# Group 0's low-part subtraction moved from VectorE to GpSimd in three of four wide expert stages

## The reference

```python
def _L2_ffn_ref(x, router_w, w1, w2, w3):        # _L3_ffn_ref is the same
    ...
    topk_probs, topk_idx = jax.lax.top_k(probs, TOP_K)      # 2 of 8 experts
    ...
    h1 = jnp.einsum('nc,ehc->neh', flat, w1)     # 64 -> 682
    h3 = jnp.einsum('nc,ehc->neh', flat, w3)
    h = jax.nn.silu(h1) * h3
    y = jnp.einsum('neh,ech->nec', h, w2)        # 682 -> 64
    out = jnp.einsum('ne,nec->nc', gates, y)
```

## Time and profile before

| | |
|---|---|
| median of 3 runs | 2331.3 us (2331.04 to 2332.63) |
| the profiled execution, its own time | 2329.65 us |
| its span | 2327.8 us |
| mean granted TensorE clock | 0.812 of full speed |
| DVE / PE / ACT / POOL busy | 74% / 68% / 58% / 43% |
| `y_done` waits of POOL (L602) | 449.3 us in 136 waits |

### The profile page before, as it was taken

The page is one execution under the profiler, slowest core; times in us unless marked ns, Lnnn a source line. Parts: engine busy times, 40 slices in busy tenths (PEclk is TensorE's granted clock), DMA queues, the critical chain, the costliest instruction groups (busy, mean ns, idle before and its releaser), DMA issues.

```text
span 2327.8 us, 50752 instructions
## 1 busy us (share of the span) xinstructions
PE 1580.9 (68%) x16748; PEld 1179.4 (51%) x16749; DVE 1718.9 (74%) x2892; ACT 1354.8 (58%) x2460; POOL 1006.3 (43%) x955
## 2 busy tenths in 40 slices
PE   4367777778676767657777912699913099977995
PEld 3344444435343433336667811688802088866884
DVE  3567668776877587547778867788867588869886
ACT  0256655677778676765656711477701277766774
POOL 1023334432223122871223478144477577754443
PEclk8578767778898677997888955799955599989997
DMA  7000000000002000000000010010020211110012
GB/s 300 0 25 1 1 25 1 1 1 1 1 1 76 23 1 5 21 26 15 17 16 22 22 59 22 20 28 27 20 84 22 91 36 34 34 63 23 26 29 88
DMA packets 53028, 76.25 MB, mean 33 GB/s; under 512 B 14905, under 2 KB 37642, under 8 KB 50206
## 3 DMA queue, kind: packets, MB, share of 16 engines
q1 hardware_dynamic: 30658, 43.26, 6.1%
q0 software_dynamic: 22208, 30.81, 3.8%
HBM read 40.89 MB, written 35.19 MB: 33 GB/s over the span
## 4 chain that ended last, share of the span: by engine, by line
PE 32%; DVE 17%; issue 6%; POOL 5%; ACT 2%; DMA 2%; POOLq 0%; SPq 0%; ACTq 0%; DVEq 0%
PE bank L1607 12%; PE bank L1608 9%; PE bank L1621 5%; POOL rows L578 3%; DVE tmp L1067 2%; PE bank L1623 2%; PE bank L1593 1%; DVE act L1227 1%; DVE hl L1231 1%; PE bank L1372 1%; POOL x L616 1%; PE bank L1503 1%; ACT act L774 1%; DVE tmp L1045 1%; DVE st L892 1%
## 5 line engine op out<-in xcount | busy, mean ns | idle before, releaser
L602 POOL DMA_INDIRECT y<-ysb,ids x352 | 394.8, 1122 | 522.6 <-DVE ysb L1218 449.3
L616 POOL TENSOR_TENSOR x<-x,ysb 128x256 f32<-128x256 f32 x288 | 267.4, 928 | 665.6 <-DVE ysb L1305 657.3
L756 ACT ACTIVATE hb<-bank,bias_sb 128x512 f32<-128x512 f32 x432 | 298.6, 691 | 244.2 <-issue 141.6
L578 POOL DMA_INDIRECT rows<-rowsb,pos x288 | 333.1, 1156 | 103.6 <-issue 74.6
L1607 PE MATMUL bank<-xT,gA 128*114 128x256 f16 x1056 | 330.6, 313 | 59.8 <-DVE act L1227 28.5
L1227 DVE TENSOR_TENSOR act<-bank,act 114x512 f32<-114x512 f32 x352 | 241.5, 686 | 162.9 <-ACT act L774 162.2
L774 ACT ACTIVATE act<-bank 114x512 f32<-114x512 f32 x352 | 210.2, 597 | 235.1 <-PE bank L1608 232.1
L1608 PE MATMUL bank<-xT,gB 128*114 128x256 f16 x1056 | 298.7, 283 | 0.0
L1607 PE MATMUL bank<-xT,uA 128*114 128x256 f16 x1056 | 298.1, 282 | 0.0
L1608 PE MATMUL bank<-xT,uB 128*114 128x256 f16 x1056 | 298.1, 282 | 0.0
L1621 PE MATMUL bank<-dW,hl 114*128 x2112 | 259.8, 224 | 7.0 <-DVE hl L1231 6.1
(11 more groups left out here) (239 smaller groups left out, 3371.2 us busy)
## 6 DMA issues: line engine op xcount, KB each, us to landing
xs<-rows SPq DMA_DIRECT2D x176, 65.0 KB
stage<-up SPq DMA_DIRECT2D x8, 1368.0 KB, 6.8
rows<-land POOLq DMA_DIRECT2D x8, 1137.5 KB, 17.8
y<-ysb,ids POOLq DMA_INDIRECT x352, 2.2
rows<-rowsb,pos POOLq DMA_INDIRECT x288, 2.4
stage<-down SPq DMA_DIRECT2D x2, 1368.0 KB
rowsb<-y SPq DMA_DIRECT2D x4, 640.0 KB, 6.2
rows<-land POOLq DMA_DIRECT2D x4, 585.0 KB, 20.6
```

The lines of the kernel that those rows point to most:

```text
L578: pool.indirect_dma_start(rows_d[l - SPARSE][h], bass.IndirectOffsetOnAxis(pos[h][:, k, j:j + 1], 0), words(h)[:, j * RW // 2:(j + 1) * RW ...
L602: pool.indirect_dma_start(y_d[h], bass.IndirectOffsetOnAxis(ids[h][:, t * SUB + u:t * SUB + u + 1], 0), ysb[t % UNROLL][:, u * C:(u + 1) * ...
L616: pool.tensor_tensor(xv, xv, tg[u % 2], ALU.add).then_inc(s["added"], 1)
L756: ins = a.activation(dst[:, 0:SPAN * P], PB[w % 3][:, :], ACT.Gelu, scale=1.0 / WSCALE, bias=b1T[l][:, at:at + 1])
```

## The change

In the stages (2,0), (2,1) and (3,1), not in (3,0), `low` of group 0 is no longer on DVE. POOL does it, in `back`: tiles 0 and 1 ahead of everything, tile t + 2 behind the two transfers of tile t. A new semaphore `helped` counts these; `silu` and `down23` of group 0 wait on it, and the counts of `hp_ready` shrink accordingly.

```diff
+        HELPED = [(2, 0), (2, 1), (3, 1)]
+        def on_pool(l, h, g):
+            return g == 0 and (l, h) in HELPED
+        def low_ready(eng, l, h, i, k, g):
+            if on_pool(l, h, g):
+                wait_from(eng, s["helped"], i * UNROLL + (help_base(l, h) + k + 1))
+            else:
+                n = lows(l, h)
+                wait_from(eng, s["hp_ready"], i * (UNROLL * n) + (split_base(l, h) + k * n + g + 1 - (SPLIT - n)))
...
             def back(l, h, aside, early):
...
+                def low(t):
+                    if on_pool(l, h, 0) and t < TILES:
+                        pool.wait_ge(s["hi_ready"], (tile_base(l, h) + t) * SPLIT + 1)
+                        pool.tensor_tensor(hl[0][0:CH, 2 * ROWS:4 * ROWS], hold(0, 0)[0:CH, :], hl[0][0:CH, 0:2 * ROWS],
+                                           ALU.subtract).then_inc(s["helped"], 1)
+                low(0)
+                low(1)
                 for t in range(TILES):
...
                     pool.wait_ge(s["y_done"], tile_base(l, h) + t + 1)
                     for u in range(SUB):
                         pool.indirect_dma_start(y_d[h], bass.IndirectOffsetOnAxis(ids[h][:, t * SUB + u:t * SUB + u + 1], 0),
...
+                    low(t + 2)
...
                 def silu(i, k, g):
-                    wait_from(a, s["hp_ready"], i * (UNROLL * SPLIT) + (sb_ + (k - 1) * SPLIT + g + 1))
+                    if not (isinstance(i, int) and i == 0 and k == 0):
+                        low_ready(a, l, h, i, k - 1, g)
...
                 def low(i, k, g):
-                    v.wait_ge(s["hi_ready"], i * (UNROLL * SPLIT) + (sb_ + k * SPLIT + g + 1))
+                    if on_pool(l, h, g):
+                        return
+                    v.wait_ge(s["hi_ready"], i * (UNROLL * SPLIT) + (hb_ + k * SPLIT + g + 1))
...
                 def down23(i, k, g, e):
-                    pe.wait_ge(s["hp_ready"], i * (UNROLL * SPLIT) + (split_base(l, h) + k * SPLIT + g + 1))
+                    low_ready(pe, l, h, i, k, g)
```

More of the change, by code:

```diff
@@ L339, in program @@
                  "bias_ld b_done l1b_ps w01_done b2_ld b2_moved "
-                 "split_lo xt_ps xt_done cnt_ps cnt_read gain_read res_read up_ps gelu_done lo_ready down_ps gated added").split()
+                 "split_lo xt_ps xt_done cnt_ps cnt_read gain_read res_read up_ps gelu_done helped lo_ready down_ps gated added").split()
         s = {n: sem(n) for n in names}
@@ L419, in middle, with lows, help_base @@
                 body(i)
-        def split_base(l, h):
-            return m_of(l, h) * TILES * SPLIT
+        HELPED = [(2, 0), (2, 1), (3, 1)]
+        def on_pool(l, h, g):
+            return g == 0 and (l, h) in HELPED
+        def lows(l, h):
+            return sum(not on_pool(l, h, g) for g in range(SPLIT))
+        def split_base(l, h):
+            return sum(TILES * lows(*divmod(m + SPARSE * HALVES, HALVES)) for m in range(m_of(l, h)))
+        def help_base(l, h):
+            return sum(TILES * (SPLIT - lows(*divmod(m + SPARSE * HALVES, HALVES))) for m in range(m_of(l, h)))
+        def low_ready(eng, l, h, i, k, g):
[4 more added lines that the diff above has]
+                wait_from(eng, s["hp_ready"], i * (UNROLL * n) + (split_base(l, h) + k * n + g + 1 - (SPLIT - n)))
         def hold(k, g):
@@ L764, in moe @@
                 gb, tb = group_base(l, h), tile_base(l, h)
-                sb_ = split_base(l, h)
                 plan = inner(l, h)
@@ L1219, in evict @@
                     ins.then_inc(s["y_done"], 1)
-                sb_ = split_base(l, h)
+                hb_ = m_of(l, h) * TILES * SPLIT
                 def product(i, k, g):
```

## The result

| | before | after |
|---|---|---|
| median of 5 runs, taken beside each other | 2331.3 us (2330.26 to 2332.63) | 2546.63 us (2538.64 to 2549.79) |
| the profiled execution, its span | 2329.65, 2327.8 us | 2546.9, 2545.1 us |
| mean granted TensorE clock | 0.812 | 0.803 |

The changed kernel takes 1.0918 times as long (95% interval 1.0903 to 1.0934), 215 us more. 2553 was forecast.

What follows compares the result with a forecast made beforehand. TensorE was taken to set the pace in the three undisturbed stretches, 485.6 us for 101 tiles. A POOL loop of 7.0 us a tile makes 707, 221 more; 2331.3 + 221 gives 2553 us, range 2496 to 2645.

Steps and rivals of the forecast that it cites:

- The loop: Three wide stages: POOL's subtraction, silu, product, eviction and both transfers run once per tile, 7.0 us against 4.66 to 4.93.
- The estimate for the subtraction: POOL's subtraction of 114 x 512 elements, estimated at 1.3 us, with ends of 0.74 and 1.90.
- leaving the exclusion out of the sum: POOL's and DVE's subtractions excluding one another: 0.37 us a tile, 7.37 and 2590 us, not taken.
- an even distance: In (2,1) and (3,1), starts of the first transfers should stand 7.0 us apart, evenly.
- The longer fourth tile: Each fourth tile's pause of some 1.3 us should fall into time in which engines wait for POOL.
- The sum: Undisturbed stretches of three stages: 101 tiles x 7.0 = 707 us in place of 485.6, so 221 more.
- Two terms set at zero: First part of (2,0): 7.3 us lacking against at most 8 won, zero; stage (3,0): keeps its length.
- DVE's relief: First part of (2,0), where DVE can be late: 14 x 0.60 = 8 us at most.
- The dearer operation: Rival: POOL's subtraction costs 1.9 us or more, giving 2613, and 2664 at 2.4 us; chance 0.12.
- The clock: Rival: TensorE falls to 1.2 GHz, 8.8 us a tile; 2735 for all 101 tiles, 2644 for half; chance 0.09.
- The loop that doesn't close: Rival: POOL's 3.9 us a tile fit into 4.66 and are hidden; time stays at 2331; chance 0.04.
- The faster case: Rival: POOL's work hidden and DVE's relief counts in the first part of (2,0), 8 us, 2323; chance 0.03.

Runs made afterwards that it cites:

- e10_lean: Against e1_ahead: `helped` rises by 3 a tile and `hp_ready` by 2 for group 1, so wait values are those of the kernel before; 2338.05 us.
- e9_counts_only: Against the kernel before: only the change's semaphores and counts, DVE still does all subtractions in the old order; 2347.31 us.
- e1_ahead: Against the changed kernel: POOL's subtraction of tile t + 2 moved ahead of the wait for `y_done` of tile t, TensorE given its own wait; 2355.62 us.
- e3_twice: Against the changed kernel: POOL's subtraction behind the transfers done twice, first into a spare tile; 2680.74 us.
- e2_between: Against the changed kernel: POOL's subtraction of tile t + 2 placed between the two transfers of tile t; 2417.16 us.
- e6_idle_work: Against the kernel before: POOL also subtracts constants into a spare tile behind the transfers in the same three stages, nobody waiting for it; 2428.13 us.
- e6w_write_only: Against e6_idle_work: a memset of 114 x 1024 fp16, which reads nothing, in place of the useless subtraction; 2338.03 us.

## Why the prediction was right

**What bounds the kernel.** Right: TensorE sets the pace before. e10_lean shows it: DVE's busy time in (2,1) fell by 20.8 us, and the stretch didn't get shorter. What the prediction left out is that TensorE's pace has an issue part: nine register operations more a pass lengthen (3,0) by 6.1 us in after and by 7.5 in e9_counts_only.

**The loop.** Right, and shown from both sides: opened, the same work costs 26 us, and 6 with lean counts (e1_ahead, e10_lean); lengthened by 1.11 us it costs 134 us more (e3_twice); shortened by one transfer and a gap it gives tiles of 5.24 (e2_between). The rows of POOL, ScalarE, DVE and TensorE follow each other as the prediction walked through them.

**Its terms.** 7.0 was forecast, 6.53 is the clean turn:

| term | forecast | measured |
|---|---|---|
| silu to product | 0.63 | 0.62 |
| product to the eviction's end | 1.63 | 1.63 |
| eviction to transfer | 0.77 | 0.77 |
| two transfers | 2.56 | 2.28 |
| transfer to subtraction | 0.03 | 0.00 |
| subtraction | 1.3 | 1.19 |
| handing on to silu | 0.10 | 0.04 |

The largest miss is in the transfers: the first one, 1.28 us in the earlier trace rows, is 1.00 in the new rhythm, where no `low` of DVE is running at its start (see the last section). The estimate for the subtraction, extended from an addition and a copy, was 0.1 too high; here the estimate after the Trainium skill, GPSIMD Engine Reference, section 3.1, 1.2 us, was the closer one. The sources of the two rows (ns min/median/max) show the operation and DVE's remaining `low`:

```profile
L623 POOL TENSOR_TENSOR hl<-act,hl x132: 1147/1190/1283, 1048.8 to 2517.9; 114x512 f16<-114x512 f32 x132
```

```profile
L1264 DVE TENSOR_TENSOR hl<-hb,hl x176: 670/681/748, 1052.0 to 2517.1; 114x512 f16<-114x512 f32 x176
```

Between 1.15 and 1.28 us in all 132: POOL is never held up. The second row is of group 2 alone. DVE's `low` of group 1 does run into POOL's subtraction, in 8 of the 41 tiles of (2,1), and is the one that is held; here POOL's began at 1657.97:

```profile
1658.23 1.48 DVE L1264 TENSOR_TENSOR hl<-act,hl 114x512 f16<-114x512 f32 x1
1659.88 0.69 DVE L1258 TENSOR_TENSOR act<-bank,act 114x512 f32<-114x512 f32 x1 [0.17 <-ACT act L805]
```

The next product, at 1659.88, still waits for silu, so it costs nothing here. So leaving the exclusion out of the sum was right, but its reason (DVE is idle when POOL's turn comes) holds only for most tiles, and e6_idle_work shows that with another phase the exclusion costs 96 us. It was a matter of phase, and the prediction could only argue it.

**Why the mean is 6.74.** The forecast was an even distance. Of the 101 tiles 51 take 6.53 to 6.60 us (but only 2 of the 19 of (2,0)); nearly all others take up to 7.1, as the turn that begins with the transfer at 1648.64 above and goes on:

```profile
1649.94 1.50 POOL L632 DMA_INDIRECT y<-ysb,ids  x1 [0.30 <-issue]
...
1649.91 0.68 DVE L1264 TENSOR_TENSOR hl<-act,hl 114x512 f16<-114x512 f32 x1
```

The second transfer takes 1.50 instead of 0.98, with DVE's subtraction running when it starts. The 101 tiles take 21.6 us more than 101 times 6.53, and 13.7 of them are lengthened transfers (some 3 of these beside DVE's joining of results in (3,1)). Some 3 more are eight turns in which silu starts 0.25 to 0.6 us behind POOL's subtraction; the one looked at is under the rivals. The longer fourth tile has shrunk to 0.06 us, as forecast.

**The sum.** 101 x 7.0 - 485.6 = 221 became 681.1 - 485.6 = 195.5 for the same tiles. Two terms set at zero made up most of the difference. The first part of (2,0) lost 14.6 us: DVE's relief gave nothing there, and `down` waited 18.7 us in 10 waits for POOL's subtraction,

```profile
PE bank L1654 <- POOL hl L623: 18.7, 10, 3.3
```

where the sum had let each tile take the longer of loop and own work; the prediction had kept 20 us for it in the range. And (3,0) was said to keep its length since its code stays. Its work does, its counts don't: 6.1 us. The total of 2553 is therefore closer than its terms deserve, 25 too many in the loop and 22 too few beside it: that these cancel is luck. The mechanism is not, nor are the steps of the ring.

**The rivals.** The dearer operation is out (1.19 us). The clock did fall, for a small part of the time: its means of 0.90 to 0.94 in the loop, 1.00 before, are means of 1.00 and 0.50, which makes some 50 of the 276.7 us of (2,1) at 1.2 GHz. Two stretches of equal length there:

```profile
1746.00:1752.80 6.80, 5.87 (x44) 5.74 (x45) 2.48 (x5) 3.40 (x8) 3.44 (x4) 0.50 0.07 20
1754.00:1760.80 6.80, 4.27 (x49) 3.57 (x48) 3.51 (x6) 3.80 (x9) 3.30 (x3) 1.00 0.07 19
```

In the first TensorE is busy 5.87 us for fewer matmuls, silu came 0.6 us late, and the tile took 7.11. The argument against this rival, that the clock had fallen around waits of twice the new pause, did not hold: TensorE's longest wait for POOL in (2,1) was 2.5 us. Its price was small, since it held for only a part of the time. The loop that doesn't close is what e1_ahead shows, in another place of the program than that of the change. The faster case is out by e10_lean.

## What to carry to other kernels

Before work is moved to an engine because that engine is idle, follow the queue of the engine it goes to: what it must wait for ahead of the new work, and whether that in its turn waits for the new work of the time before; if it does, each step of the ring is paid in each turn, and the fix is the place (ahead of the wait), not the engine. Relief for an engine that isn't the one waited for is worth nothing, here 20.8 us of DVE's work for 0 us. And where TensorE runs a loop with little slack, counts that differ from those already in registers cost time of their own, also in stages whose work is unchanged.

## What the runs showed of the hardware

**Register operations on TensorE are on the path.** Nine more in a pass of four tiles made it 0.62 to 0.75 us longer, 0.07 to 0.08 each, with no matmul changed ((3,0) in after and e9_counts_only; back to 19.05 a pass in e10_lean). I had counted an altered wait as free.

**Two operations with two SBUF operands each, on DVE and POOL, exclude each other, and the meeting can lock in.** DVE's 0.68 us became 1.65 in the median of 41 tiles and up to 1.79 (e6_idle_work), while a memset of 0.99 us did nothing (e6w_write_only). Which of the two is held is not simply the one that the records have as the later: in 18 of the 41 tiles DVE's begins up to 0.05 us ahead of POOL's and is the one that takes 1.76 to 1.79. What I had not expected is that they meet in tile after tile.

**The issue of an indirect transfer that begins while such a DVE operation runs is drawn out to about 0.86 us behind the end of that operation.** In the earlier trace rows DVE's `low` ends at 1592.90 + 0.68 = 1593.58 and the transfer of 1.28 us at 1593.16 + 1.28 = 1594.44; in the turn above they end at 1650.59 and 1651.44. Where POOL's subtraction holds DVE's, the transfer is still tied to the end of DVE's: in the rows of e2_between DVE's 1.44 us end at 1603.66, the transfer of 1603.27 at 1604.53. So the length depends on when the transfer begins: one that starts late in the `low` would end later than that anyway and keeps its 0.98. In (2,1) before, all 84 transfers begin during a `low`; 49 take over 1.05 us, and these end 0.85 to 0.87 behind it. In (2,1) after, 25 of 84 do; 17 are longer, with 0.85 to 0.87, and the 8 that are not began within 0.03 us of DVE's start. None of the other 59 is longer. That is a relation in time over many rows; no run took the one away to see the other go.
